# First-choice flags and destinations of the expert tiles' rows made by GpSimd, three small operations a tile, in place of VectorE

## The reference

```python
logits = xf @ router_w
gate_vals, idx = jax.lax.top_k(logits, 2)
gates = softmax(gate_vals)
for e in range(8):
    h = relu(xf @ w1[e] + b1[e]) @ w2[e] + b2[e]
    y = layernorm(xf + h, gamma[e], beta[e])
    out += where(idx == e, gates, 0).sum(-1)[:, None] * y
```

## Time and profile before

| | us |
|---|---|
| median of 3 runs | 539.31 (539.29 to 540.76) |
| the profiled execution | 539.75 |
| its span, first to last instruction | 538.0 |
| PE busy | 482.5 (90%) |
| DVE busy | 440.2 (82%) |
| ACT busy | 366.8 (68%) |
| POOL busy | 307.6 (57%) |

### The profile page before, as it was taken

One profiled execution on the slowest core, in us unless ns is written; L12 is line 12 of the kernel. 1 busy time (PEld: TensorE's weight loads), 2 busy tenths in 40 slices (PEclk: granted clock), 3 DMA queues, 4 the chain that ended last, 5 costly groups with the idle time before them and its releaser, 6 DMA issues.

```text
span 538.0 us, 15851 instructions
## 1 busy us (share of the span) xinstructions
PE 482.5 (90%) x4764; PEld 389.4 (72%) x4764; DVE 440.2 (82%) x1768; ACT 366.8 (68%) x849; POOL 307.6 (57%) x447
## 2 busy tenths in 40 slices
PE   3989999999999999989999899999999999999700
PEld 2866666767666666666666699999899999999700
DVE  5876877997777697978778669989998888879897
ACT  5566567776756767667577566876686787778562
POOL 2542021557784386576876768777776555545420
PEclk9999999999899999999899999999999999999955
DMA  5247744426154322333311674877897788886499
GB/s 148 76 153 234 232 108 136 125 81 190 34 174 125 115 88 93 108 110 116 124 37 33 175 262 132 220 201 208 245 275 234 210 244 244 248 225 213 151 337 260
DMA packets 73590, 90.43 MB, mean 168 GB/s; under 512 B 9262, under 2 KB 57297, under 8 KB 73506
## 3 DMA queue, kind: packets, MB, share of 16 engines
q1 hardware_dynamic: 52626, 66.43, 43.0%
q0 software_dynamic: 6416, 12.93, 6.8%
q10 hardware_dynamic: 14464, 10.06, 6.2%
HBM read 63.25 MB, written 30.79 MB: 175 GB/s over the span
## 4 chain that ended last, share of the span: by engine, by line
PE 36%; issue 21%; POOL 20%; DVE 14%; ACT 3%; DMA 2%; SPq 1%; ACTq 1%; POOLq 0%; DVEq 0%
PE sbk L985 12%; POOL sorted_d L1685 11%; PE avb L997 6%; PE mbk L997 6%; POOL kept L1662 2%; POOL rs L1671 2%; PE mbk L975 1%; PE mbk L860 1%; PE avb L800 1%; DVE stk L1575 1%; PE sbk L827 1%; DMA xins<-in_xp 1%; PE gen L808 1%; DVE pexs L1457 1%; DVE pexs L1487 1%
## 5 line engine op out<-in xcount | busy, mean ns | idle before, releaser
L1685 POOL DMA_INDIRECT sorted_d<-pay,slot x96 | 96.8, 1008 | 35.8 <-issue 25.1
L1188 DVE TENSOR_REDUCE mx<-mbk 128x4 f32<-128x768 f32 x96 | 91.1, 949 | 30.3 <-PE mbk L860 29.9
L1699 POOL DMA_INDIRECT expert_d<-pexs,dest x70 | 70.3, 1004 | 42.6 <-DVE pexs L1487 24.8
L648 ACT ACTIVATE pexs<-sbk 128x768 f32<-128x768 f32 x96 | 77.5, 808 | 22.7 <-PE sbk L887 21.2
L985 PE MATMUL sbk<-pexs 128*128 128x256 f32 (+1 forms) x224 | 50.6, 369 | 0.3 <-ACT pexs L697 0.3
L985 PE MATMUL sbk<-pexs,stk 128*128 128x256 f32 (+1 forms) x224 | 48.3, 358 | 1.2 <-issue 1.1
L697 ACT ACTIVATE pexs<-sbk,xins 128x256 f32<-128x256 f32 (+1 forms) x112 | 43.9, 463 | 7.8 <-PE sbk L985 5.7
L697 ACT ACTIVATE pexs<-sbk,w12s 128x256 f32<-128x256 f32 (+1 forms) x112 | 42.6, 450 | 8.2 <-PE sbk L985 6.9
L1699 POOL DMA_INDIRECT expert_d<-xT,dest x33 | 32.9, 996 | 21.4 <-issue 10.7
L985 PEld LDWEIGHTS sbk<-pexs 128*128 128x128 f32 x224 | 39.0, 190 | 4.4 <-issue 0.5
L1648 POOL TENSOR_TENSOR kept<-hs,lnb 128x384 f32<-128x384 f32 x16 | 16.0, 1000 | 45.2 <-DVE hs L1163 45.1
(11 more groups left out here) (259 smaller groups left out, 1239.5 us busy)
## 6 DMA issues: line engine op xcount, KB each, us to landing
stk<-pack_d SPq DMA_DIRECT2D x28, 512.0 KB
pexs<-pack_d SPq DMA_DIRECT2D x28, 512.0 KB
stack_d<-kqs ACTq DMA_DIRECT2D x48, 192.0 KB, 2.6
stk<-stack_d SPq DMA_DIRECT2D x64, 144.0 KB
xn<-sorted_d SPq DMA_DIRECT2D x47, 132.0 KB
pack_d<-in_w SPq DMA_DIRECT2D x16, 256.0 KB
xins<-in_xp SPq DMA_DIRECT2D x16, 128.0 KB, 3.9
hs<-in_txt SPq DMA_DIRECT2D x16, 128.0 KB, 3.2
```

The costliest lines, as they stand in the source:

```text
L648: act.activation(pex[p % 2][m][:, :, :], sbk[:, :, 0:COLS], ACT.Exp, scale=0.25).then_inc(a_pex, 1)
L1188: dve.tensor_reduce(dst, mbk[:, :, 0:COLS].rearrange("p h (c s) -> p h c s", c=2), AX.X, ALU.max).then_inc(d_mx, 1)
L1685: pool.indirect_dma_start(sorted_d[:, :], bass.IndirectOffsetOnAxis(ap=slot[p % 6][:, 2 * k + w:2 * k + w + 1], axis=0), pay[p % 6][:, k, ...
L1699: pool.indirect_dma_start(expert_d[:, :], bass.IndirectOffsetOnAxis(ap=dest[fin % DESTS][:, k:k + 1], axis=0), ye[fin % RESULTS][:, k, :], ...
```

## The change

GpSimd makes `first` and `dest` in a new function `mark(g)`, which its `step_b` calls for tile `fin` + 1 ahead of the scatters of tile `fin`. DVE's two operations and the semaphore `b_first` are gone. `b_dest` now counts three for a tile. SP's wait in `load(g)` for `dest` of tile g - 6 is kept with the new count. ACT's `norm_row(g)` gets a wait for `dest` of tile g - 4, because GpSimd reads `nr` and `xs` now.

```diff
@@ SP, load(g)
                 after(sp, b_z, g - 6)
-                after(sp, b_dest, g - 6)
+                after(sp, b_dest, g - 6, 3)
@@ ACT, norm_row(g)
                 after(act, b_y, g - NORMS)
+                after(act, b_dest, g - NORMS, 3)
@@ DVE, step_b(old, fin)
-                    after(dve, b_dest, old - 1)
-                    dve.tensor_scalar(first[:, 0:n], xs[old % 6][:, 0:n, D + 1], nr[old % NORMS][:, AT_ID:AT_ID + 1], None,
-                                      ALU.is_equal).then_inc(b_first, 1)
-                    after_scatters(old - DESTS)
-                    dve.wait_ge(b_first, old + 1)
-                    dve.scalar_tensor_tensor(out=dest[old % DESTS][:, 0:n], in0=first[:, 0:n], scalar=-float(TOKENS),
-                                             in1=xs[old % 6][:, 0:n, D], op0=ALU.mult, op1=ALU.add).then_inc(b_dest, 1)
@@ POOL
+            def mark(g):
+                if g < GRID:
+                    n = chunks(g)
+                    after_dma(pool, xs_in, g)
+                    pool.wait_ge(b_nr, g + 1)
+                    after(pool, b_dest, g - 1, 3)
+                    pool.tensor_scalar(first[:, 0:n], xs[g % 6][:, 0:n, D + 1], nr[g % NORMS][:, AT_ID:AT_ID + 1], -float(TOKENS),
+                                       ALU.is_equal, ALU.mult).then_inc(b_dest, 1)
+                    pool.wait_ge(b_dest, 3 * g + 1)
+                    pool.tensor_tensor(target[:, 0:n], first[:, 0:n], xs[g % 6][:, 0:n, D], ALU.add).then_inc(b_dest, 1)
+                    if g >= DESTS:
+                        pool.wait_ge(ye_out[(g - DESTS) % RESULTS], 16 * blocks_to(g - DESTS, chunks(g - DESTS) - 1, RESULTS))
+                    pool.wait_ge(b_dest, 3 * g + 2)
+                    pool.tensor_copy(dest[g % DESTS][:, 0:n], target[:, 0:n]).then_inc(b_dest, 1)
+
             def step_b(old, fin):
+                if 0 <= fin + 1 < GRID:
+                    mark(fin + 1)
                 if 0 <= old < ROOT:
@@ POOL, the scatters of tile fin
-                    pool.wait_ge(b_dest, fin + 1)
+                    pool.wait_ge(b_dest, 3 * fin + 3)
```

More of the change, by code:

```diff
@@ L360, in early_fusion @@
         first = sb("first", [P, 2])
+        target = sb("target", [P, 2])
         dest = ring("dest", DESTS, [P, 2], U32)
@@ L402, in early_fusion @@
         b_z, b_bn, b_mv, b_ve, b_sd, b_rs = [sem(n) for n in ("b_z", "b_bn", "b_mv", "b_ve", "b_sd", "b_rs")]
-        b_first, b_dest, b_xb, b_zg, b_y = [sem(n) for n in ("b_first", "b_dest", "b_xb", "b_zg", "b_y")]
+        b_dest, b_xb, b_zg, b_y = [sem(n) for n in ("b_dest", "b_xb", "b_zg", "b_y")]
         c_in, c_first, c_sum, c_out = sems("c_in", len(PIECES)), sem("c_first"), sem("c_sum"), sem("c_out")
```

## The result

The median is 586.94 us (586.07 to 587.61); the kernel before took 540.03 us beside it (539.29 to 542.87). The ratio is 1.0857, with a 95% interval of 1.0812 to 1.0902. The forecast was 550.1 (545 to 558): the direction was right, and the loss is four times the size. No rival reached it either.

The account below looks back on a forecast made before the run. PE was taken to bound stage B, with GpSimd's queue full from tile 3's to tile 19's scatters. A delay of 11.2 us less 0.4 of DVE relief, on 539.75, gave 550.55, as median 550.1 (545 to 558).

Parts of the forecast that it names:

- the price of a mark: GpSimd's queue: a mark between two transfers adds 0.70 us, bounds 0.46 to 1.1.
- The gap of 0.17 us: GpSimd's queue: the next transfer starts 0.17 us after a small operation ends, in place of 0.30.
- from tile 20 on the delay stands: Without sends GpSimd needs about 3.3 us a tile, PE 3.73, so the delay stops growing at tile 25 or so.
- about 2: GpSimd's queue without sends: a tile of 128 rows with its mark takes about 2 us.
- The push: GpSimd's queue: marks ahead of tile 19's first scatter delay it by 14.1 us.
- Marks 1 to 3: GpSimd, ahead of the power of tiles 1 to 3: no gap saved, about 0.85 us each.
- The path: PE's product waits for turning, SP's load and GpSimd's mark: delay 1.0 us at tile 9, 11.2 at tile 25.
- the landing: SP's load of 132 KB, between mark and turning: taken as 3.0 us.
- After tile 28 the marks fall into idle time: GpSimd's queue: after tile 28 each step has idle time, which takes in the marks.
- Rival 1: DVE holds up GpSimd's small operations: a mark costs 1.1 us, total about 558; chance 0.14.
- Rival 2: Marks fill gaps between GpSimd's transfers: a mark costs 0.46 us or less, total about 545; chance 0.10.
- Rival 3: GpSimd's delay is hidden below 0.16 us a mark; DVE's relief returns 1.2 and 0.4 us: 537.7; chance 0.04.

Follow-up runs that it names:

- e6_wait3: e5_free3 with one wait more, the third operation waiting for the second: 583.50 us, ratio 1.0792.
- e5_free3: Kernel before plus three unused mark-like GpSimd operations a tile, without waits between them or the third's wait for scatters: 556.82 us, ratio 1.0294.
- e9_late: Changed kernel, but DVE makes flags and destinations of tiles 0 to 20, GpSimd only those of tiles 21 to 55: 560.89 us, ratio 1.0365.
- e4_spread: Changed kernel with marks two tiles ahead, their three operations spread before, between and behind the scatters: 558.96 us, ratio 1.0324.
- e1_mock: Kernel before plus three unused GpSimd operations a tile, with the real mark's waits among them: 587.89 us, ratio 1.0845.
- e7_one_dve: Kernel before with flag and destination made in one DVE operation, GpSimd left alone, results read back in 512-byte pieces: 543.76 us, ratio 1.0054.
- e2_ahead: Changed kernel with marks made two tiles ahead of their scatters, not one: 588.76 us, ratio 1.0868.

## Why the prediction was wrong, step by step

**The failed step is the price of a mark: 0.70 us taken, 1.40 measured, above even the upper bound of 1.1.** Term by term, in the order of the prediction's sum (medians of after, 395 to 500 us, from start to start):

| term | taken | measured |
|---|---|---|
| transfer's end to the comparison | 0.01 | 0.08 |
| comparison to addition | 0.32 | 0.39 |
| addition to copy, with a wait | 0.27 | 0.33 |
| copy and gap to the transfer | 0.19 + 0.17 | 0.19 + 0.62 |
| the first transfer itself, longer | 0 | 0.09 |
| the gap saved | -0.30 | -0.30 |
| for the third wait and the scalar | 0.04 | in the rows above |

The gap of 0.17 us was taken from behind an operation of 0.97 us, not behind a short one. The kernel before had the right row, in GpSimd's timeline, and I didn't read it:

```profile
314.95 0.19 POOL L1673 TENSOR_TENSOR nm<-ve,rs 128x3 f32<-128x3 f32 x1
315.76 1.09 POOL L1685 DMA_INDIRECT sorted_d<-pay,slot  x1 [0.62 <-issue]
```

A short operation that had waited for its predecessor, and a transfer 0.81 us behind its start, which itself takes 1.09. With this row the price is 0.01 + 0.32 + 0.27 + 0.81 + 0.12 - 0.30 = 1.23: over the threshold that comes next. The same queue has the other case too, a copy that waits for nothing just issued:

```profile
280.75 0.20 POOL L1677 COPY pay<-tok 128x3 f32<-128x3 f32 x1
281.12 0.98 POOL L1685 DMA_INDIRECT sorted_d<-pay,slot  x1 [0.16 <-issue]
```

So the length of the operation alone doesn't make the gap; the wait ahead of it does, as e6_wait3 shows beside e5_free3.

**What the size turned over: "from tile 20 on the delay stands".** This needed a mark below 3.73 - 2.58 = 1.15 us. At 1.40 to 1.43 GpSimd is slower than PE on every full tile, sends or none, and far slower on half tiles, for which "about 2" was taken and 2.67 measured, beside PE's 1.87. From the first scatter of tile 3 to that of tile 55 the queue's sum is 43 x 4.0 + 9 x 2.67 + 14 x 1.29 = 214 us; the trace has 216.1 (346.60 to 562.73), before it was 174.9. e9_late shows this part alone: 20 us. Even near the old price some of it was left out (3.6 us in e4_spread): a half tile with a mark of 0.78 us would be 2.05, above 1.87, and e4_spread's took 2.44 (median), with addition and copy in a row.

**The push.** Scatters of tile 19 begin 27.5 us later (428.85 against 401.35), 25.7 without the start's shift; 14.1 was forecast. Marks 1 to 3 cost the 0.85 taken (346.60 - 340.87 = 5.7, less 1.8 and 1.40, is 2.5, by difference); marks 5 to 20 took 21.8 us, 1.36 each. Only the size was wrong: with 1.40 in place of 0.70 the prediction's own sum gives 3 x 0.85 + 17 x 1.40 - 0.32 - 2.9 = 23.1 us at tile 25, where 21.8 were measured.

**The path was right for PE, and the time didn't hang on it.** Loads behind the marks, from tile 9 on (0.8 us late beyond the shift; 1.0 forecast), a tight chain from mark to product. Its latency was 2.8 us, not 3.4: the landing took 2.3 and not 3.0, the median of the group too:

```profile
xn<-sorted_d SPq DMA_DIRECT2D x47, 132.0 KB, 2.3
```

But e1_mock shows that the path wasn't needed: without it the full queue comes through the `ye` ring, the last send and the reading back, in the same total. The prediction named the first two and priced neither; the third, which waits for tile 51's scatters, it left out.

**The end.** "After tile 28 the marks fall into idle time" was wrong: GpSimd is still 7.9 us behind DVE at tile 50 and 6.4 at tile 53, the results come back later, and ACT's `weighted(0)`, which stands ahead of the root of tile 54 in its queue, waits 7.0 us for rows. With it 6.1 us were left out.

**Rival 1** had a price of 1.1 for a mark, nearest to the truth, by the wrong mechanism. DVE's interference is small: the comparison's median of 307 ns is next to its minimum of 301, the maximum 668; over the three operations together means exceed medians by 0.08 us. The mark at 491.71 us ran while DVE was idle (491.42 to 492.84) and shows the usual starts, 0.39, 0.33 and 0.80 us apart. The exclusive lock of the Trainium skill, "SBUF — State Buffer", section "SBUF: two separate sides", would explain single slow ones, and neither the 0.62 us nor any part of the mark's median. **Rival 2**, the filled gap, fell: the gap behind a short operation grew. **Rival 3** kept its one true part, the 1.2 us (e7_one_dve). Its limit of 0.16 us a mark is a tenth of what a mark takes.

## What to carry to other kernels

Price a small operation on a queue of transfers by what lies from its start to the next transfer's start, read behind an operation of the same length and with the same wait; the operations' own time was 0.69 of 1.40 us here. Then compare the new step with the step of the engine that sets the pace, for each size of tile, before saying that a delay stops growing: a queue that is full at 76% busy (26.76 of 35 us) has nothing to give. Then ask what waits for that queue last: here the reading back behind tile 51. Where operations must go there, wait only for what was issued a transfer earlier (e4_spread against the change: 28 us; making the marks a tile earlier, e2_ahead, gave none of it).

## What the runs showed of the hardware

**A wait on the engine's own last operation, ahead of a short one, holds the transfer behind it.** The transfer starts 0.78 us after the short operation does, 0.34 without the wait (e6_wait3 against e5_free3), and behind waits met long ago the gap is 0.17 to 0.28 (e4_spread). That GpSimd's sequencer prepares a transfer while the operations ahead still run, and can't get ahead of an open wait, fits all these rows; it is argued, not shown by itself. The transfer behind the three operations also takes 1.06 us in place of 0.97, with the waits (after) or without them (e5_free3), but 0.98 behind the single copy at 280.75; why stays open.

**PE's granted clock falls when it waits long.** In e1_mock PE waits 10.81 us for tile 28. Timeline of PE, and the windows after that wait (columns as in the earlier trace rows):

```profile
432.86 0.69 PE L976 MATMUL mbk<-ident,xn 128*128 128x128 f32 x2 [10.81 <-DMA xn<-sorted_d]
433.35 3.62 PE L986 MATMUL sbk<-pexs,stk 128*128 128x256 f32 x8
```

```profile
433.00:436.70 3.70, 3.70 (x10) 3.04 (x11) 0.00 (x0) 1.23 (x3) 2.61 (x5) 0.50 0.97 294
437.00:441.00 4.00, 4.00 (x24) 3.87 (x24) 1.29 (x6) 1.88 (x6) 2.78 (x6) 0.75 0.98 353
```

The clock is at 0.50 (1.2 GHz) and eight products take 3.62 us in place of 1.89; it is 0.75 on average from 437 to 441, and 1.00 (2.4 GHz) from 441 to 445. The short waits for loads in the changed kernel, up to 1.7 us each, left it at 1.00 in both of its windows. A wait of 2.51 us for ACT's turned rows, which ended at 355.31, was followed by 3.4 us at 0.50, in which eight products took 3.63 us, 1.7 more than at 1.00. The clock is no cause of the 47 us: e1_mock, at 0.50 for 13.7 us around tile 28, starts the scatters of tile 51 within 0.2 us of the changed kernel's.
